# Rotary sum on GpSimd instead of VectorE, and the scaling of the keys at the end of VectorE's iteration

## The chip, the cores and the metric

One core of one Trainium2 chip runs the kernel. The metric is the device time of one execution in microseconds (us). The kernel before was run three times: 747.37 us is the median, 747.22 the lowest and 750.02 the highest.

## What is computed

The kernel is one decoder layer over 32 sequences of 112 rows of 256 numbers. It has three blocks, each with a layer norm before it and a residual sum behind it: attention with 8 heads of 128, attention-like weighing of a context of 375 rows with a gelu, and a quantised feed-forward block with 1,024 hidden units. The change touches the attention:

```python
q = _rmsnorm(einsum('bim,mhd->bhid', x, wq)); k = _rmsnorm(einsum('bim,mhd->bhid', x, wk))
even, odd = split(q, 2, axis=-1)            # the same for k
q = concatenate([even * cos - odd * sin, even * sin + odd * cos], axis=-1)
s = einsum('bhid,bhjd->bhij', q * mult, k * mult)
```

The norm of a head is one factor for each row and head, so the kernel turns first and scales afterwards.

## The kernel before, in words

One sequence is one unit of work, and four sequences are in flight. Each engine has its own hand-written program. `iterations` (line 252) runs its `body(i)` 35 times: three special first ones (FIRST, SECOND, THIRD), a loop unrolled by four, and a drain. Within an iteration, `a` is the sequence whose projections are made, `b` the one before it (scores, softmax, values, output projection), `c` the one before that (context and hidden units), `d` the oldest (its last product), `n` and `m` the next two. Every engine works through its list strictly in order, so a wait holds all that is behind it. The engines are tied together by semaphores only.

The way of the keys `k` of sequence `a` (w = 1; the queries are w = 0):

- TensorE projects them (line 909) into the banks `k_ps`. ScalarE squares them (line 718), and VectorE sums the squares by head (`sum_squares`, line 474, in two halves for the keys).
- VectorE multiplies by the cosines (`turn_cos`, line 482, into `turn_c`) and, with the halves swapped, by the sines (`turn_sin`, line 491, into `turn_s`). `turn` (line 498) adds both into `turn_c`: 112 partitions x 1,024 numbers.
- GpSimd turns the sums of squares into factors in `rms_root` (line 349 adds the epsilon, line 351 raises to -0.5).
- VectorE scales the keys in `normalise_k` (line 503). ScalarE scales the queries in `normalise_q` (line 774) in two halves of four instructions each.
- At the start of the next iteration TensorE waits in `transpose_qk` (line 914) for the scaled queries, transposes their eight heads (line 917), waits for the scaled keys (`k_normed`) and transposes theirs. Only then does it begin the next projection.

The end of an iteration, engine by engine. TensorE ends with `project_out(range(HH, H), b)` (line 1094), twelve products (line 876), the last of which raises `y_ready`. VectorE ends with `split_oT(1, b)` (line 557), `turn(1, a)` (line 662), `split_xnT(n)` (line 433), `normalise_k(a)` (line 666), `residual_attention(b)` (line 568, which waits for `y_ready`; its sum is line 570), `layer_stats` for `b` and `m` (lines 402 to 415) and `clip_hidden(c)` (line 564). GpSimd's order in an iteration is `split_ctx(c)` (line 355), `mask_later_keys(b)` (line 367), `rms_root(0, a)`, `root(2, c)` (line 344), `rms_root(1, a)`, `add_b2(c)` (line 360), `root(1, b)` and `root(0, m)`. The middle of VectorE's iteration has `gelu_outer(c)` (line 515), `turn(0, a)` (line 638), `split_g(c)` (line 530), `turn_cos(1, a)`, ..., where `split_g` waits for a copy by ScalarE and gives TensorE the input of `ctx_out(c)`.

The loads and stores go through SyncE's queue: it stores `y_out` after `out_done`, loads a context after `ctx_lo_done` and a block of x after `x2_done`. No DMA is issued from GpSimd's or VectorE's queue.

Of the kernel before, what the change touches and what calls it, by code (L numbers as in the profile page):

```python
# [29 lines left out]
ALU = mybir.AluOpType  # L30
# [38 lines left out]
def done(j):  # L69

    return j.base + j.off + 1
# [12 lines left out]
def decoder_layer(nc, x, ctx_rows, wq, wk, wv, wo, w1, b1, w2, b2, tables, out):  # L84
# [15 lines left out]
    with ExitStack() as stack:  # L100
# [224 lines left out]
        @block.gpsimd  # L325
        def _(pool):
            pool.memset(nhalf[:, :], -0.5).then_inc(const_done, 1)
            pool.memset(ln_eps[:, :], LN_EPS).then_inc(const_done, 1)
            pool.memset(rms_eps[:, :], RMS_EPS / QK_LIFT ** 2).then_inc(const_done, 1)
            pool.memset(v_sb[:, :, D:VW], 1.0).then_inc(const_done, 1)  # L330
            pool.memset(pool_cell[:, :], 0.0).then_inc(const_done, 1)
            pool.wait_ge(const_done, 5)

            def carry_wait():

                pool.tensor_tensor(pool_cell[:, :], pool_cell[:, :], pool_cell[:, :], ALU.mult)

            def root(n, j):

                if n < 2:  # L340
                    pool.wait_ge(mv_done[n], done(j))
                    pool.tensor_tensor(ve[n][:, :], mv[n][:, 1:2], ln_eps[:, :], ALU.add).then_inc(ve_done[n], 1)
                pool.wait_ge(ve_done[n], done(j))
                pool.tensor_tensor(rstd[n][:, :], ve[n][:, :], nhalf[:, 0:1], ALU.pow).then_inc(rstd_done[n], 1)  # L344

            def rms_root(w, j):

                pool.wait_ge(qk_summed[w], done(j))
                pool.tensor_tensor(ms[:, w, :], ss[:, w, :], rms_eps[:, :], ALU.add).then_inc(qk_ms_done[w], 1)
                pool.wait_ge(qk_ms_done[w], done(j))  # L350
                pool.tensor_tensor(rms[:, w, :], ms[:, w, :], nhalf[:, 0:H], ALU.pow).then_inc(qk_rms_done[w], 1)  # L351

            def split_ctx(j):
                pool.wait_ge(ctx_hi_done, done(j))
                pool.tensor_tensor(ctx_lo[:, :, :], ctx_in[:, j.off % 2], ctx_hi[:, :, :].bitcast(F32),  # L355
                                   ALU.subtract).then_inc(ctx_lo_done, 1)

            def add_b2(j):
                pool.wait_ge(x3_done, done(j))
                pool.tensor_tensor(x3b[:, :], x3[:, :], b2_rows[:, :], ALU.add).then_inc(x3b_done, 1)  # L360

            def mask_later_keys(j):

                pool.wait_ge(exp_done, done(j))
                carry_wait()
                p = p_sb.rearrange("k (h t) -> k h t", h=H)
                pool.affine_select(out=p, in_=p, compare_op=ALU.is_ge, fill=0.0, base=0,
                                   pattern=[[0, H], [1, T]], channel_multiplier=-1).then_inc(p_done, 1)

            def body(i):  # L370
                a, b, c, d, n, m = i, i.plus(-1), i.plus(-2), i.plus(-3), i.plus(1), i.plus(2)
                A, B_, C, D_, N, M_ = (j.inside(B) for j in (a, b, c, d, n, m))
                if i is FIRST:
                    root(0, n)
                if B_ and not A:
                    mask_later_keys(b)
                if C:
                    split_ctx(c)
                if B_ and A:
                    mask_later_keys(b)  # L380
                if A:
                    rms_root(0, a)
                if C:
                    root(2, c)
                if A:
                    rms_root(1, a)
                if C:
                    add_b2(c)
                if B_:
                    root(1, b)  # L390
                if M_:
                    root(0, m)

            iterations(pool, body)


        @block.vector
        def _(dve):
# [92 lines left out]
                dve.tensor_tensor(turn_s[:, w, :].rearrange("t (h two f) -> t h two f", two=2, f=HALF),  # L491
                                  halves, table, ALU.mult).then_inc(sin_done[w], 1)

            def turn(w, j):

                dve.wait_ge(cos_done[w], done(j))
                dve.wait_ge(sin_done[w], done(j))
                dve.tensor_tensor(turn_c[:, w, :], turn_c[:, w, :], turn_s[:, w, :], ALU.add).then_inc(qk_turned[w], 1)  # L498

            def normalise_k(j):  # L500
                dve.wait_ge(k_turned, done(j))
                dve.wait_ge(k_rms_done, done(j))
                dve.tensor_tensor(heads(qkn[:, 1, :]), heads(turn_c[:, 1, :]),
                                  rms[:, 1, :].unsqueeze(2).broadcast_to([T, H, D]), ALU.mult).then_inc(k_normed, 1)
# [75 lines left out]
            def body(i):  # L580
                a, b, c, d, n, m = i, i.plus(-1), i.plus(-2), i.plus(-3), i.plus(1), i.plus(2)
                A, B_, C, D_, N, M_ = (j.inside(B) for j in (a, b, c, d, n, m))
                if i is FIRST:
                    wait_x(n)
                    layer_stats(x_rows(n))
                    normalise_x(n)
                    split_xnT(n)
                    for w in range(3):
                        split_projection(w)
                    dve.wait_ge(ident_in, 16)  # L590
                    dve.tensor_copy(ident_b[:, :], ident[:, :]).then_inc(ident_b_done, 1)
                    wait_x(m)
                    layer_stats(x_rows(m))
                    return
                if i is SECOND:
                    normalise_x(n)
                    dve.wait_ge(table_in, 32)
                    turn_cos(0, a)
                    turn_sin(0, a)
                    sum_squares(0, a).then_inc(q_summed, 1)  # L600
                    split_xnT(n)
                    turn(0, a)
                    sum_squares(1, a).then_inc(k_summed, 1)
                    turn_cos(1, a)
                    turn_sin(1, a)
                    turn(1, a)
                    normalise_k(a)
                    clip_weights(0)
                    return
                if B_:  # L610
                    split_qkT(0, b)
                if i is THIRD:
                    split_wo(0)
                if C and A:
                    normalise_x2(c)
                if B_:
                    split_qkT(1, b)
                if C and not A:
                    normalise_x2(c)
                if i is THIRD:  # L620
                    wait_x(n)
                    layer_stats(x_rows(n))
                    clip_weights(1)
                    fixed_biases()
                if D_:
                    residual_out(d)
                if A:
                    turn_cos(0, a)
                    turn_sin(0, a)
                    sum_squares(0, a).then_inc(q_summed, 1)  # L630
                if C:
                    gelu_inner(c)
                if N:
                    normalise_x(n)
                if C:
                    gelu_outer(c)
                if A:
                    turn(0, a)
                if C:
                    split_g(c)  # L640
                if A:
                    turn_cos(1, a)
                if B_:
                    invert_sums(b)
                if A:
                    turn_sin(1, a)
                if i is THIRD:
                    split_wo(1)
                if C:
                    residual_ctx(c)  # L650
                if A:
                    sum_squares(1, a, slice(0, HH))
                if B_:
                    split_oT(0, b)
                if C:
                    quantise_x3(c)
                if A:
                    sum_squares(1, a, slice(HH, H)).then_inc(k_summed, 1)
                if B_:
                    split_oT(1, b)  # L660
                if A:
                    turn(1, a)
                if N:
                    split_xnT(n)
                if A:
                    normalise_k(a)
                if B_:
                    residual_attention(b)
                if M_:
                    wait_x(m)  # L670
                if B_:
                    dve.wait_ge(x2_done, done(b))
                if B_ or M_:
                    layer_stats(*([x2_rows(b)] if B_ else []), *([x_rows(m)] if M_ else []))
                if C:
                    clip_hidden(c)

# [448 lines left out]
```

## Time and profile before

| what | value |
|---|---|
| median of three runs (lowest, highest) | 747.37 us (747.22, 750.02) |
| span of the profiled execution | 745.4 us |
| TensorE matmuls busy | 714.9 us, 96% |
| VectorE busy | 655.2 us, 88% |
| ScalarE busy | 548.8 us, 74% |
| GpSimd busy | 308.1 us, 41% |
| mean granted clock of TensorE | 0.985 |

The span goes from the first to the last instruction of the one execution that was profiled. Its own total is not given beside it; the median of the runs is 1.97 us above the span. In the rows below PE is TensorE's matmul side, PEld its weight loads, DVE VectorE, ACT ScalarE and POOL GpSimd. L909 is line 909. The granted clock is a share of full speed: 1.00 is 2.4 GHz, 0.50 is 1.2 GHz.

### The profile page before, as it was taken

What the parts mean: (1) busy time and instruction counts of PE and PEld (TensorE: products, weight loads), DVE (VectorE), ACT (ScalarE), POOL (GpSimd) and SP (SyncE); (2) the same over time, 40 slices, a digit from 0 to 9 for tenths busy, and PEclk for the clock granted to TensorE, in tenths of its full rate; (3) what the DMA queues carried; (4) which work ended last, traced back from release to release, by engine and by line L of the source; (5) the groups of instructions that cost most, each with busy time, mean ns of one, the idle gap of its engine ahead of it and who ended that gap; (6) DMA issues with size and microseconds to landing.
All of it is one profiled execution on the core that took longest, in us unless ns stands there. A gap on an engine that the chain in (4) does not pass through costs nothing.

```text
span 745.4 us, 15919 instructions
## 1 busy us (share of the span) xinstructions
PE 714.9 (96%) x5824; PEld 633.9 (85%) x5824; DVE 655.2 (88%) x1264; ACT 548.8 (74%) x1324; POOL 308.1 (41%) x425
## 2 busy tenths in 40 slices
PE   5799999999999999999999999999999999999974
PEld 4588988888888989898898989889898988889863
DVE  6989989999999999999999999999999999998942
ACT  5777777778777777787777878777787777778752
POOL 1335434543443453344344344444434444443421
PEclk9799999999999999999999999999999999999996
DMA  7400011100101100000110000101000011100000
GB/s 264 157 8 28 28 36 34 31 17 28 33 27 33 33 24 21 27 31 29 33 33 19 26 27 27 33 33 33 15 30 27 27 33 34 33 11 20 28 7 12
DMA packets 15371, 26.58 MB, mean 36 GB/s; under 512 B 1536, under 2 KB 10192, under 8 KB 15216
## 3 DMA queue, kind: packets, MB, share of 16 engines
q1 hardware_dynamic: 15344, 26.22, 10.7%
q8 instruction: 17, 0.28, 0.2%
q14 instruction: 10, 0.08, 0.0%
HBM read 22.55 MB, written 3.67 MB: 35 GB/s over the span
## 4 chain that ended last, share of the span: by engine, by line
PE 90%; DVE 3%; ACT 3%; issue 2%; DMA 1%; POOL 1%; SPq 0%; POOLq 0%; DVEq 0%; ACTq 0%
PE psum L909 34%; PE psum L876 22%; PE psum L937 7%; PE psum L917 6%; PE psum L982 6%; PE psum L1013 4%; PE psum L1005 3%; PE psum L944 3%; PE psum L972 3%; PE psum L965 2%; DMA w_raw<-in_wv 1%; ACT qkn L774 1%; ACT w_raw L764 1%; PE psum L997 1%; DVE qkT_lo L550 0%
## 5 line engine op out<-in xcount | busy, mean ns | idle before, releaser
L909 PE MATMUL psum<-wqkv_hi,xnT_hi 128*112 128x512 f32 x384 | 159.3, 415 | 4.4 <-DVE wqkv_lo L440 2.7
L909 PE MATMUL psum<-wqkv_lo,xnT_hi 128*112 128x512 f32 x384 | 151.3, 394 | 0.0
L909 PE MATMUL psum<-wqkv_hi,xnT_lo 128*112 128x512 f32 x384 | 131.8, 397 | 0.0
L344 POOL TENSOR_TENSOR rstd<-ve,nhalf 112x1 f32<-112x1 f32 x96 | 55.4, 577 | 145.8 <-DVE ve L414 140.8
L351 POOL TENSOR_TENSOR rms<-ms,nhalf 112x8 f32<-112x8 f32 x64 | 107.2, 1676 | 5.0
L718 ACT ACTIVATE sq<-psum 112x1024 f32<-112x1024 f32 x64 | 65.0, 1016 | 56.4 <-PE psum L909 56.4
L355 POOL TENSOR_TENSOR ctx_lo<-ctx_in,ctx_hi 125x768 fp32r<-125x768 f32 x32 | 58.6, 1830 | 95.9 <-ACT ctx_hi L684 95.9
L764 ACT ACTIVATE w_raw<-psum,rden 112x128 f32<-112x128 f32 x256 | 69.7, 384 | 26.6 <-DVE rden L525 26.5
L909 PEld LDWEIGHTS psum<-wqkv_hi,xnT_lo 128*112 128x112 f32 x384 | 67.3, 175 | 22.4
L909 PEld LDWEIGHTS psum<-wqkv_hi,xnT_hi 128*112 128x112 f32 x384 | 67.7, 176 | 19.8 <-issue 3.1
L774 ACT ACTIVATE qkn<-turn_c,rms 112x128 f32<-112x128 f32 x256 | 81.5, 400 | 1.4 <-POOL rms L351 1.4
L474 DVE TENSOR_REDUCE ss<-sq 112x4 f32<-112x512 f32 (+1 forms) x95 | 81.8, 861 | 0.0
L909 PEld LDWEIGHTS psum<-wqkv_lo,xnT_hi 128*112 128x112 f32 x384 | 67.9, 177 | 15.1
L482 DVE TENSOR_TENSOR turn_c<-psum,cos_t 112x1024 f32<-112x1024 f32 x64 | 77.8, 1216 | 2.2 <-ACT sq L718 2.2
L876 PE MATMUL psum<-wo_hi,oT_hi 128*112 128x256 f32 x256 | 78.8, 308 | 0.8 <-DVE oT_lo L557 0.8
L498 DVE TENSOR_TENSOR turn_c<-turn_c,turn_s 112x1024 f32<-112x1024 f32 x64 | 77.9, 1217 | 0.1
L491 DVE TENSOR_TENSOR turn_s<-psum,sin_t 112x1024 f32<-112x1024 f32 x64 | 77.3, 1208 | 0.0
L876 PE MATMUL psum<-wo_lo,oT_hi 128*112 128x256 f32 x256 | 72.1, 282 | 0.0
L876 PE MATMUL psum<-wo_hi,oT_lo 128*112 128x256 f32 x256 | 71.8, 281 | 0.0
L550 DVE TENSOR_TENSOR qkT_lo<-psum,qkT_hi 128x896 f16<-128x896 f32 x64 | 69.2, 1082 | 0.2 <-ACT qkT_hi L684 0.2
L788 ACT ACTIVATE f_int<-psum,b_col 128x112 int16<-128x112 f32 x256 | 65.9, 371 | 1.8 <-PE psum L1005 1.8
L937 PE MATMUL psum<-v_sb,w_raw 112*112 112x129 f32 x512 | 62.0, 273 | 0.0
(99 smaller groups left out, 1792.2 us busy)
## 6 DMA issues: line engine op xcount, KB each, us to landing
ctx_in<-in_ctx_rows SPq DMA_DIRECT2D x32, 375.0 KB
x_in<-in_x SPq DMA_DIRECT2D x32, 112.0 KB, 2.0
out_y<-y_out SPq DMA_DIRECT2D x32, 112.0 KB, 1.9
w_raw<-in_w SPq DMA_DIRECT2D x2, 1024.0 KB, 6.2
w_raw<-in_wq SPq DMA_DIRECT2D x2, 512.0 KB, 4.5
w_raw<-in_wk SPq DMA_DIRECT2D x2, 512.0 KB, 6.1
w_raw<-in_wv SPq DMA_DIRECT2D x2, 512.0 KB, 7.8
w_raw<-in_wo SPq DMA_DIRECT2D x1, 1024.0 KB, 10.3
```

The costliest lines, as they stand in the source:

```text
L351: pool.tensor_tensor(rms[:, w, :], ms[:, w, :], nhalf[:, 0:H], ALU.pow).then_inc(qk_rms_done[w], 1)
L474: return dve.tensor_reduce(ss[:, w, hs], heads(sq[:, w, :])[:, hs, :], AX_X, ALU.add)
L482: dve.tensor_tensor(turn_c[:, w, :].rearrange("t (b h d) -> t b h d", b=2, d=D), (q_ps, k_ps)[w].rearrange("t b (h d) -> t b h d", d=D), c ...
L491: dve.tensor_tensor(turn_s[:, w, :].rearrange("t (h two f) -> t h two f", two=2, f=HALF), halves, table, ALU.mult).then_inc(sin_done[w], 1)
L498: dve.tensor_tensor(turn_c[:, w, :], turn_c[:, w, :], turn_s[:, w, :], ALU.add).then_inc(qk_turned[w], 1)
L550: dve.tensor_tensor(qkT_lo[:, w, :].rearrange("p (b n) -> p b n", b=2), (qT_ps, kT_ps)[w], qkT_hi[:, w, :].rearrange("p (b n) -> p b n", b=2),
L764: last = act.activation(on[:, h * D:(h + 1) * D], o_ps[:, h // OH, (h % OH) * VW:(h % OH) * VW + D], ACT.Copy, scale=rden[:, h:h + 1])
L774: last = act.activation(qkn[:, 0, h * D:(h + 1) * D], turn_c[:, 0, h * D:(h + 1) * D], ACT.Copy, scale=rms[:, 0, h:h + 1])
L788: last = act.activation(f_int[:, c * T:(c + 1) * T], f_ps[:, c // (FC // 2), (c % (FC // 2)) * T:(c % (FC // 2) + 1) * T], ACT.Relu, bias= ...
L876: product = pe.matmul(dst, lh, rh, start=first and k == 0, stop=last and k == len(terms) - 1)
L909: last = pe.matmul(ps[:, n, :], left[:, c, :], right[:, c, w, n * BANK:(n + 1) * BANK], start=c == 0 and left is xnT_hi and right is wqkv_ ...
L937: last = pe.matmul(o_ps[:, h // OH, at:at + VW], p_sb[:, h * T:(h + 1) * T], v_sb[:, h, :], start=h % OH == 0, stop=h % OH == OH - 1 or h ...
```

## The change

The function `turn` moves from VectorE's program to GpSimd's. GpSimd calls it for the queries behind `rms_root(0, a)` and for the keys behind `rms_root(1, a)`. VectorE's calls go. `normalise_k(a)` moves from its place before `residual_attention(b)` to the place behind `layer_stats` and before `clip_hidden(c)`. In the special iteration SECOND only the calls of `turn` go. TensorE's, ScalarE's and SyncE's programs stay as they are. The diff:

```diff
--- before.py
+++ after.py
@@ -343,6 +343,12 @@
                 pool.wait_ge(ve_done[n], done(j))
                 pool.tensor_tensor(rstd[n][:, :], ve[n][:, :], nhalf[:, 0:1], ALU.pow).then_inc(rstd_done[n], 1)
 
+            def turn(w, j):
+
+                pool.wait_ge(cos_done[w], done(j))
+                pool.wait_ge(sin_done[w], done(j))
+                pool.tensor_tensor(turn_c[:, w, :], turn_c[:, w, :], turn_s[:, w, :], ALU.add).then_inc(qk_turned[w], 1)
+
             def rms_root(w, j):
 
                 pool.wait_ge(qk_summed[w], done(j))
@@ -380,10 +386,12 @@
                     mask_later_keys(b)
                 if A:
                     rms_root(0, a)
+                    turn(0, a)
                 if C:
                     root(2, c)
                 if A:
                     rms_root(1, a)
+                    turn(1, a)
                 if C:
                     add_b2(c)
                 if B_:
@@ -490,12 +498,6 @@
                 table = sin_t[:, :].rearrange("t (two f) -> t two f", two=2).unsqueeze(1).broadcast_to([T, H, 2, HALF])
                 dve.tensor_tensor(turn_s[:, w, :].rearrange("t (h two f) -> t h two f", two=2, f=HALF),
                                   halves, table, ALU.mult).then_inc(sin_done[w], 1)
-
-            def turn(w, j):
-
-                dve.wait_ge(cos_done[w], done(j))
-                dve.wait_ge(sin_done[w], done(j))
-                dve.tensor_tensor(turn_c[:, w, :], turn_c[:, w, :], turn_s[:, w, :], ALU.add).then_inc(qk_turned[w], 1)
 
             def normalise_k(j):
                 dve.wait_ge(k_turned, done(j))
@@ -599,11 +601,9 @@
                     turn_sin(0, a)
                     sum_squares(0, a).then_inc(q_summed, 1)
                     split_xnT(n)
-                    turn(0, a)
                     sum_squares(1, a).then_inc(k_summed, 1)
                     turn_cos(1, a)
                     turn_sin(1, a)
-                    turn(1, a)
                     normalise_k(a)
                     clip_weights(0)
                     return
@@ -634,8 +634,6 @@
                     normalise_x(n)
                 if C:
                     gelu_outer(c)
-                if A:
-                    turn(0, a)
                 if C:
                     split_g(c)
                 if A:
@@ -658,12 +656,8 @@
                     sum_squares(1, a, slice(HH, H)).then_inc(k_summed, 1)
                 if B_:
                     split_oT(1, b)
-                if A:
-                    turn(1, a)
                 if N:
                     split_xnT(n)
-                if A:
-                    normalise_k(a)
                 if B_:
                     residual_attention(b)
                 if M_:
@@ -672,6 +666,8 @@
                     dve.wait_ge(x2_done, done(b))
                 if B_ or M_:
                     layer_stats(*([x2_rows(b)] if B_ else []), *([x_rows(m)] if M_ else []))
+                if A:
+                    normalise_k(a)
                 if C:
                     clip_hidden(c)
 
```

## Rows read from the trace of the kernel before

**Rows 1.** The page: span, busy times, and the granted clock in 40 slices.

```profile
span 745.4 us, 15919 instructions
...
PE 714.9 (96%) x5824; PEld 633.9 (85%) x5824; DVE 655.2 (88%) x1264; ACT 548.8 (74%) x1324; POOL 308.1 (41%) x425
...
PEclk9799999999999999999999999999999999999996
```

**Rows 2.** The chain that ended last, its longest pieces: start, duration, work.

```profile
384.91 2.79 PE psum L909 x12
406.77 2.79 PE psum L909 x12
```

**Rows 3.** Groups of instructions: busy us, mean ns of one, idle before it.

```profile
L498 DVE TENSOR_TENSOR turn_c<-turn_c,turn_s 112x1024 f32<-112x1024 f32 x64 | 77.9, 1217 | 0.1
...
L355 POOL TENSOR_TENSOR ctx_lo<-ctx_in,ctx_hi 125x768 fp32r<-125x768 f32 x32 | 58.6, 1830 | 95.9 <-ACT ctx_hi L684 95.9
...
L360 POOL TENSOR_TENSOR x3b<-x,b_rows 112x256 f32<-112x256 f32 x32 | 23.6, 737 | 0.0
```

**Rows 4.** Line 503 alone: shortest, median and longest ns, first and last start.

```profile
L503 DVE TENSOR_TENSOR qkn<-turn_c,rms x32: 1212/1540/1689, 26.5 to 703.6; 112x1024 f32<-112x1024 f32 x32
```

**Rows 5.** Timeline of TensorE where one iteration ends: start, duration, instruction.

```profile
420.37 0.28 PE L876 MATMUL psum<-wo_hi,oT_lo 128*112 128x256 f32 x1
...
420.38 1.60 PEld L917 LDWEIGHTS psum<-ident,qkn 112*128 112x128 f32 x16
```

**Rows 6.** Timeline of VectorE at the same iteration's end.

```profile
419.48 1.53 DVE L503 TENSOR_TENSOR qkn<-turn_c,rms 112x1024 f32<-112x1024 f32 x1
420.94 0.41 DVE L570 TENSOR_TENSOR x<-psum,x_in 112x256 f32<-112x256 f32 x1
...
422.34 0.43 DVE L564 TENSOR_SCALAR f_q<-f_int 128x448 bf16<-128x448 int16 x2
```

**Rows 7.** Timeline of GpSimd at the same iteration's end.

```profile
417.58 1.65 POOL L351 TENSOR_TENSOR rms<-ms,nhalf 112x8 f32<-112x8 f32 x1
419.20 0.73 POOL L360 TENSOR_TENSOR x3b<-x,b_rows 112x256 f32<-112x256 f32 x1
```

**Rows 8.** Timeline at VectorE's wait for TensorE, in the drain.

```profile
723.68 0.28 PE L876 MATMUL psum<-wo_hi,oT_lo 128*112 128x256 f32 x1
...
723.99 0.42 DVE L570 TENSOR_TENSOR x<-psum,x_in 112x256 f32<-112x256 f32 x1 [2.86 <-PE psum L876]
```

**Rows 9.** Timeline of the same iteration's middle: GpSimd, VectorE, TensorE's loads, ScalarE.

```profile
408.70 1.65 POOL L351 TENSOR_TENSOR rms<-ms,nhalf 112x8 f32<-112x8 f32 x1
...
409.33 0.49 ACT L684 ACTIVATE g_hi<-g 125x336 fp32r<-125x336 f32 x1 [0.57 <-DVE g L515]
...
410.35 0.50 DVE L530 TENSOR_TENSOR g_lo<-g,g_hi 125x336 fp32r<-125x336 f32 x1
...
411.71 0.17 PEld L876 LDWEIGHTS psum<-ctx_hi,g_hi 125*112 125x112 f32 x1
...
415.77 1.27 ACT L774 ACTIVATE qkn<-turn_c,rms 112x128 f32<-112x128 f32 x4
```

**Rows 10.** Timeline of the special iteration SECOND: the queries' root and their scaling.

```profile
20.68 2.58 POOL L351 TENSOR_TENSOR rms<-ms,nhalf 112x8 f32<-112x8 f32 x1
...
23.35 2.45 ACT L774 ACTIVATE qkn<-turn_c,rms 112x128 f32<-112x128 f32 x8 [1.43 <-POOL rms L351]
```

**Rows 11.** TensorE's stops: timeline, with the idle time before in brackets.

```profile
20.67 0.49 PE L909 MATMUL psum<-wqkv_hi,xnT_hi 128*112 128x512 f32 x1 [1.63 <-DVE xnT_lo L433]
...
25.94 1.58 PE L917 MATMUL psum<-ident,qkn 112*128 112x112 f32 x8 [2.23 <-ACT qkn L774]
...
732.25 0.37 PE L876 MATMUL psum<-ctx_hi,g_hi 125*112 125x256 f32 x1 [3.19 <-DVE g_lo L530]
```

**Rows 12.** Stretches of 0.25 us: busy by engine, then granted clock (PEclk).

```profile
26.00:26.25 0.25, 0.25 (x3) 0.25 (x4) 0.25 (x1) 0.25 (x1) 0.00 (x0) 0.73 0.32 123
...
36.25:36.50 0.25, 0.25 (x7) 0.25 (x5) 0.25 (x1) 0.00 (x0) 0.25 (x2) 0.79 0.00 0
```

## The prediction

> **What bounds the kernel now.** I read the page first. TensorE's matmul side is busy 96% of the span, VectorE 88%, GpSimd 41%, and the granted clock stands at nine tenths or more in all slices but one [rows 1]. The chain that ended last says the same: its longest piece, the twelve products of the key projection, returns after 406.77 - 384.91 = 21.86 us [rows 2], and the pieces between are TensorE's too. So an iteration lasts as long as TensorE's list, which runs there without a stop. VectorE saves nothing by being faster unless TensorE waits for it, and anything that makes TensorE stop is added in full.
>
> The next view is the timeline at the end of one iteration. TensorE's last output product starts at 420.37 and ends at 420.65; its weight loads for the 16 transposes follow at once, from 420.38 to 421.98 [rows 5]. The first eight are the queries', so the keys' begin at 420.38 + 1.60 / 2 = 421.18. VectorE had scaled the keys from 419.48 to 421.01, before it took the residual sum at 420.94 [rows 6]. The scaled keys are just there when TensorE wants them.
>
> **Removed: two sums on VectorE.** They are 64 instructions of 1,217 ns, 77.9 us in all, 2.43 us per iteration [rows 3]. On the path that sets the end they are worth nothing, since the steady iteration has no stop of TensorE for VectorE to shorten. The freed time becomes waiting.
>
> **Added: two sums on GpSimd.** No row has this size. Two sums and differences of the same engine are near: 768 columns take 1,830 ns and 256 take 737 ns [rows 3]. The slope is (1,830 - 737) / 512 = 2.13 ns per column, so 1,024 columns take 1,830 + 256 x 2.13 = 2,376 ns; in plain proportion to the larger row it would be 2,440 ns. I take 2.38 us. That is 152 us more for GpSimd, 460 us of some 745, so it does not become the bound by its total.
>
> For the queries, the root ends at 408.70 + 1.65 = 410.35, the sum at 412.7, and ScalarE begins to scale them at 415.77 [rows 9]: hidden, with 3 us to spare. For the keys, the root ends at 417.58 + 1.65 = 419.23 and the sum at 421.61 [rows 7]. Behind it stand `add_b2` and both last roots. The roots need statistics that end near 422.1 even now, so they move by the 0.73 us of `add_b2` [rows 7] at most, and what they feed (`normalise_x2`, then `normalise_x`) is not wanted by TensorE until after its next projection. I cost that at nothing.
>
> **Moved: the scaling of the keys.** This is the term that counts. Behind `layer_stats`, it stands behind `residual_attention`, whose wait is for TensorE's last product of the iteration. So the chain is closed: TensorE ends its list, VectorE does the residual sum, statistics and scaling, and TensorE, having transposed the queries, must wait for it. Step by step:
>
> - VectorE starts the residual sum 0.03 us after the product's end, as it did in the drain, where it was really waiting (723.68 + 0.28 = 723.96, start 723.99) [rows 8]. Here: 420.68.
> - From the start of that sum to the start of what follows the statistics takes 422.34 - 420.94 = 1.40 us [rows 6]. The scaling starts at 422.08. GpSimd's sum, done at 421.61, is 0.47 us early.
> - The scaling takes 1.21 us at least, 1.54 in the median and 1.69 at most [rows 4]. The instance at 419.48 took 1.53, and GpSimd's `add_b2` ran beside it until 419.93 [rows 6, 7]: 0.45 us beside each other cost 0.32. After the change `add_b2` runs from 421.61 to 422.34, beside the scaling for 0.26 us, so I take 1.21 + 0.19 = 1.40. It ends at 423.48, and with 0.03 us for the release TensorE goes on at 423.51.
>
> The stop is 423.51 - 421.18 = 2.33 us. The bounds are 2.14 us (scaling 1.21) and 2.62 us (1.69). It comes at the start of every iteration whose keys were scaled in the new place, sequences 1 to 31: 31 x 2.33 = 72 us, between 66 and 81. Nothing wins it back, since TensorE's list has no other stop. `clip_hidden`, queued behind the scaling, is 1.4 us later against TensorE, but is first wanted after the next projection. No DMA moves; SyncE's waits are for results ahead of the scaling.
>
> The Trainium skill, on the page "SBUF — State Buffer" in the section "SBUF: two separate sides", says that GpSimd and a VectorE instruction with two SBUF inputs take turns on a shared pair of ports, and that the later one is held until the other's whole instruction is done. By that, the scaling would start only at 422.34 and run 1.21 us, and the stop would be 2.40 us instead of 2.33; the slow instance above agrees with it roughly (held 0.32 us where the rule says 0.45).
>
> **The start.** In SECOND both sums go before the first key and query transposes. There the queries' root took 2.58 us from 20.68 and ScalarE began at 23.35 [rows 10]. I take 1.65 us for the root now that no sum on VectorE runs beside it, then 2.38: 24.71, some 1.4 us later; with the root still at 2.58 it would be 2.3 us. The keys' sum is another GpSimd sum behind. I take 2 us for the start, between 1 and 4.
>
> **The clock.** The stops that matter are long for it. TensorE stopped for 2.23 us before 25.94 [rows 11], and the granted clock went from 1.00 to 0.50 in the stretch after 26.00, to come back only in the one after 36.25 [rows 12]. A stop of 1.63 us before 20.67 brought no fall; one of 3.19 us in the drain, before 732.25, did [rows 11], by the last slice of the page. The new stop lies at the edge. [...] How many stops bring a fall these rows don't say: between none and 31, so 0 to 56 us. Since the two stops over 2.2 us did and the 1.63 us one did not, and the new one is barely over, I take one in five: 6 x 1.8 = 11 us.
>
> **The sum.** On the profiled execution: 745.4 + 72 + 2 + 11 = 830.4 us of span. The median of the runs is 1.97 us above that span, so the time is 832.5 us.
>
> **The rivals.**
>
> 1. *The clock falls in most iterations.* For it: both stops over 2.2 us were followed by a fall [rows 11, 12]. Against it: they are two, in the start and the drain, with other stops near them, while here 22 us of full work surround each. All 31 give 821.5 + 56 = 877 us, half of them 849. Chance 0.24.
> 2. *GpSimd's sum of the queries holds VectorE.* ScalarE's copy of `g_hi` ends at 409.82, and `split_g` waited until 410.35 only because the sum was before it on VectorE [rows 9]. Now it can start at 409.85, half a microsecond before GpSimd's sum at 410.35. If the order turns round and the sum holds it until 412.7, it ends at 413.2, where TensorE wants it at 411.71 [rows 9]: a second stop of 1.5 us, 31 x 1.5 = 47 us on 821.5 to 832.5, some 870 to 880. The page named above is the rule by which it would. It decides from a delay of 0.5 us. Chance 0.05.
> 3. *GpSimd's sum of the keys is the late one.* Its cover is 422.08 - 419.23 = 2.85 us. If the sum takes 3.6 us, as it would if VectorE slowed it by half, each stop grows by 0.8 us: 25 us more, 857 us. Chance 0.05.
> 4. *The other side: no slower, or faster.* This needs the scaling to end before 421.18, that is to start by 420.0, while its queue is held until 420.68. Then only the relief of VectorE would be left, and what it can win is the two stops of TensorE behind VectorE in the start and drain, 1.63 and 3.19 us [rows 11]: 747.4 - 4.8 = 742.6 us. For it speaks only that VectorE is at 88%. Chance 0.03.
>
> **How the numbers follow.** The forecast, a stop of 2.1 to 2.6 us with few falls, has 0.63 and its own range 813 to 850. Rival 1 fills 849 to 880, where rivals 2 and 3 lie too. The range from 812 to 880 leaves out rival 4 and the tails, under 2 in 10. About 0.5% is what a measurement can tell from no change: faster by more than that 0.02, within it 0.01, slower 0.97.
>
> **What would show it.** TensorE idle before a line 917 load in each iteration, released by VectorE's line 503, some 2.3 us and 31 times; line 498 on GpSimd near 2.4 us; VectorE idle before line 570 for TensorE; the distance of the projections near 24.2 us where the clock stands at full. More than ten stretches of clock 0.50 in the body would show rival 1, an idle TensorE before the context products rival 2, and line 503 released by GpSimd rival 3. A steady distance still near 21.9 us would prove me wrong altogether.

## The result and the profile after

The changed kernel takes 824.06 us in the median of four runs (822.43 to 825.46), against 747.3 us for the kernel before. The ratio is 1.1023, with a 95% interval of 1.0996 to 1.105: it is 10% slower. The profiled run took 825.35 us, its span 823.6.

These lines of the page answer to [rows 1 and 3]. The last two come from the full list of groups of instructions (out<-in, shapes, count, busy us, mean ns, idle before it and its releaser).

```profile
span 823.6 us, 15919 instructions
...
PE 728.9 (88%) x5824; PEld 639.5 (78%) x5824; DVE 587.2 (71%) x1200; ACT 551.8 (67%) x1324; POOL 493.3 (60%) x489
...
PEclk9899999999999999999999999999999999999995
...
PE 80%; DVE 11%; issue 3%; POOL 2%; ACT 2%; DMA 1%; SPq 0%; POOLq 0%; DVEq 0%
...
L350 POOL TENSOR_TENSOR turn_c<-turn_c,turn_s 112x1024 f32<-112x1024 f32 x64 | 153.7, 2402 | 0.0
L913 PEld LDWEIGHTS psum<-ident,qkn 112*128 112x128 f32 x512 | 53.3, 144 | 74.7 <-DVE qkn L505 69.1 <-issue 5.6
L505 DVE TENSOR_TENSOR qkn<-turn_c,rms 112x1024 f32<-112x1024 f32 x32 | 41.0, 1281 | 5.2 <-POOL turn_c L350 5.2
```

VectorE lost 68 us of busy time, and TensorE fell from 96% busy to 88%. The fourth line is the chain that ended last, by engine: VectorE now holds 11% of it, where it held 3%. The row to see is the second last. The loads of the transposes waited 69.1 us for the scaled keys (line 505 is the old line 503). The kernel before has 0.3 us there. Its two lines are:

```profile
PE 90%; DVE 3%; ACT 3%; issue 2%; DMA 1%; POOL 1%; SPq 0%; POOLq 0%; DVEq 0%; ACTq 0%
...
L917 PEld LDWEIGHTS psum<-ident,qkn 112*128 112x128 f32 x512 | 52.3, 143 | 3.7 <-issue 3.3 <-DVE qkn L503 0.3
```

How this looks within an iteration stands in its timeline. The first fence is VectorE's, the second GpSimd's, the third the loads of TensorE. They answer to [rows 5 to 7].

```profile
392.92 0.42 DVE L572 TENSOR_TENSOR x<-psum,x_in 112x256 f32<-112x256 f32 x1 [2.25 <-PE psum L872]
...
394.34 1.27 DVE L505 TENSOR_TENSOR qkn<-turn_c,rms 112x1024 f32<-112x1024 f32 x1
395.54 0.45 DVE L566 TENSOR_SCALAR f_q<-f_int 128x448 bf16<-128x448 int16 x2
```

```profile
391.46 2.39 POOL L350 TENSOR_TENSOR turn_c<-turn_c,turn_s 112x1024 f32<-112x1024 f32 x1
393.81 0.73 POOL L366 TENSOR_TENSOR x3b<-x,b_rows 112x256 f32<-112x256 f32 x1
394.49 1.54 POOL L342 TENSOR_TENSOR ve<-mv,ln_eps 112x1 f32<-112x1 f32 x1
```

```profile
392.61 0.83 PEld L913 LDWEIGHTS psum<-ident,qkn 112*128 112x128 f32 x8
395.67 0.78 PEld L913 LDWEIGHTS psum<-ident,qkn 112*128 112x128 f32 x8 [2.23 <-DVE qkn L505]
...
419.75 0.78 PEld L913 LDWEIGHTS psum<-ident,qkn 112*128 112x128 f32 x8 [2.20 <-DVE qkn L505]
```

VectorE had nothing to do for 2.25 us, since it waited for TensorE's last output product. Then the residual sum, 1.42 us to the scaling's start (394.34 - 392.92), 1.27 us of scaling, and 0.06 us later TensorE goes on. Each waits for the other, one after the other. From one key transpose to the next it is 419.75 - 395.67 = 24.08 us. Before, an iteration was 21.86 to 21.87 us [rows 2], so the stop adds 2.21 us.

The granted clock, read in stretches of 0.8 us: the kernel before has no stretch below 1.00 between 36.8 and 732.0. The changed one has five short ones in the body, from about 53.6, 77.6, 128.8, 347.2 and 589.6, each some 3.4 us at 0.50. Two stretches of the first (busy times by engine, then PEclk):

```profile
54.40:55.20 0.80, 0.80 (x3) 0.60 (x2) 0.37 (x1) 0.40 (x1) 0.00 (x0) 0.50 0.00 0
56.80:57.60 0.80, 0.80 (x4) 0.55 (x4) 0.00 (x0) 0.00 (x0) 0.00 (x0) 0.72 0.00 0
```

TensorE is fully busy in both, the first at half rate and the second while the clock comes back. At 1.2 instead of 2.4 GHz, 3.4 us would do the work of 1.7. What a fall cost can be measured: with the one at 347.2, it is 371.60 - 345.98 = 25.62 us from one load of the keys' transposes to the next, against 24.08 without. So a fall costs 1.54 us.

**Where the 78.2 us of span went.** The residual sum (line 570 before, 572 after) divides both spans. From its first to its last instance it was 673.9 us before and is 751.1 us now: 77.2 more. The 31 stops make 69.1 us of it (most are of 2.21 us, four of 2.31 to 2.49) and the five falls 5 x 1.54 = 7.7, together 76.8. Before the first instance it is 0.3 us less (50.1, now 49.8), behind the last 1.3 us more (21.4, now 22.7).

### The profile page after: what moved, and what is told of

It is laid out like the page before. It is cut to its first block, busy times and chain, and to the rows that moved or that the text cites. A ratio compares the mean times of both kernels' runs of the same rounds, so it can differ in the third digit from the quotient of the medians.

```text
span 823.6 us, 15919 instructions
## 1 busy us (share of the span) xinstructions
PE 728.9 (88%) x5824; PEld 639.5 (78%) x5824; DVE 587.2 (71%) x1200; ACT 551.8 (67%) x1324; POOL 493.3 (60%) x489
## 4 chain that ended last, share of the span: by engine, by line
PE 80%; DVE 11%; issue 3%; POOL 2%; ACT 2%; DMA 1%; SPq 0%; POOLq 0%; DVEq 0%
PE psum L905 31%; PE psum L872 20%; PE psum L933 7%; PE psum L978 5%; DVE qkn L505 5%; PE psum L913 4%; PE psum L1009 3%; PE psum L1001 3%; PE psum L940 3%; PE psum L968 2%; DVE stat L413 2%; DVE x L572 2%; PE psum L961 1%; DMA w_raw<-in_wv 1%; POOL turn_c L350 1%
## 5 line engine op out<-in xcount | busy, mean ns | idle before, releaser
L905 PE MATMUL psum<-wqkv_hi,xnT_hi 128*112 128x512 f32 x384 | 162.4, 423 | 4.1 <-DVE wqkv_lo L448 2.7
L905 PE MATMUL psum<-wqkv_lo,xnT_hi 128*112 128x512 f32 x384 | 154.8, 403 | 0.0
L350 POOL TENSOR_TENSOR turn_c<-turn_c,turn_s 112x1024 f32<-112x1024 f32 x64 | 153.7, 2402 | 0.0
L905 PE MATMUL psum<-wqkv_hi,xnT_lo 128*112 128x512 f32 x384 | 133.6, 402 | 0.0
L913 PE MATMUL psum<-ident,qkn 112*128 112x112 f32 x512 | 63.6, 269 | 67.5 <-DVE qkn L505 63.9
L913 PEld LDWEIGHTS psum<-ident,qkn 112*128 112x128 f32 x512 | 53.3, 144 | 74.7 <-DVE qkn L505 69.1
L357 POOL TENSOR_TENSOR rms<-ms,nhalf 112x8 f32<-112x8 f32 x64 | 105.5, 1648 | 5.0
L680 ACT ACTIVATE qkT_hi<-psum 128x896 f16<-128x896 f32 x64 | 60.0, 937 | 66.3 <-PE psum L913 66.2
L905 PEld LDWEIGHTS psum<-wqkv_hi,xnT_lo 128*112 128x112 f32 x384 | 69.2, 180 | 23.5
L905 PEld LDWEIGHTS psum<-wqkv_hi,xnT_hi 128*112 128x112 f32 x384 | 69.1, 180 | 20.2 <-issue 3.1
```

The source lines that it names most:

```text
L350: pool.tensor_tensor(turn_c[:, w, :], turn_c[:, w, :], turn_s[:, w, :], ALU.add).then_inc(qk_turned[w], 1)
L905: last = pe.matmul(ps[:, n, :], left[:, c, :], right[:, c, w, n * BANK:(n + 1) * BANK], start=c == 0 and left is xnT_hi and right is wqkv_ ...
L913: last = pe.transpose((qT_ps, kT_ps)[w][:, h // HH, (h % HH) * T:(h % HH + 1) * T], qkn[:, w, h * D:(h + 1) * D], ident[0:T, 0:T])
```

## The experiments

All ratios are to the kernel before, on the same chip. The theory was that the loss is the closed chain from TensorE's last product to the keys' transposes. The rivals were GpSimd's sums as the cost, VectorE's relief as a gain, and the clock.

### One part alone

**The move without GpSimd.**

```diff
+                if A:
+                    normalise_k(a)      # before clip_hidden(c); its call before residual_attention(b) goes
```

> Both sums stay on VectorE; only the scaling of the keys moves behind the statistics. Theory (the loss is the closed chain from TensorE's last product over residual sum, statistics and scaling to the keys' transposes): the stop is again 1.42 us to the scaling's start, 1.22 to 1.25 us of scaling and 0.05 of release, 2.2 us, and the time 820 to 827 us with 4 to 7 falls of the clock. Rival (the sums on GpSimd cost most of it): under 785 us. Rival (the clock alone): the stop remains but no falls: 815 us.

Measured: 817.14 us, ratio 1.094 (1.0922 to 1.0958). VectorE and TensorE's loads in its timeline:

```profile
413.40 0.42 DVE L570 TENSOR_TENSOR x<-psum,x_in 112x256 f32<-112x256 f32 x1 [1.13 <-PE psum L876]
...
414.82 1.20 DVE L503 TENSOR_TENSOR qkn<-turn_c,rms 112x1024 f32<-112x1024 f32 x1
...
416.08 0.78 PEld L917 LDWEIGHTS psum<-ident,qkn 112*128 112x128 f32 x8 [2.16 <-DVE qkn L503]
```

The stop is 2.16 us and there are four falls in the body of the profiled execution. The time came 3 us under the range I had given. The move alone makes 70 of the 77 us. The part of the change that has to do with GpSimd is not needed for the loss.

**GpSimd's sums without the move.**

```diff
# the changed kernel, with normalise_k(a) before residual_attention(b) again
```

> Both sums on GpSimd, the scaling of the keys at its old place, before the residual sum. Theory: the scaling now waits for GpSimd's sum, done about 2.4 us after the keys' root; TensorE would have gone on at 1.2 us before that sum's end in the old timing, so a stop of 1.7 us or more per iteration: 800 us without falls of the clock. If add_b2, which GpSimd begins in the same moment, holds the scaling as it did in the kernel before, the stop is 2.2 us: 815 to 825 us. Rival (VectorE's relief pays and only the move hurts): 742 to 750 us.

Measured: 822.09 us, ratio 1.101 (1.0991 to 1.1028). Its GpSimd and VectorE:

```profile
410.49 2.38 POOL L350 TENSOR_TENSOR turn_c<-turn_c,turn_s 112x1024 f32<-112x1024 f32 x1
412.84 0.73 POOL L366 TENSOR_TENSOR x3b<-x,b_rows 112x256 f32<-112x256 f32 x1
```

```profile
412.91 1.73 DVE L505 TENSOR_TENSOR qkn<-turn_c,rms 112x1024 f32<-112x1024 f32 x1 [3.19 <-POOL turn_c L350]
```

The stop is 2.19 us, now set by GpSimd: VectorE waits 3.19 us for the keys' sum. And the scaling takes 1.73 us instead of 1.2, because `add_b2` on GpSimd began 0.07 us before it. So either part of the change alone costs nearly what both cost together. They overlap: with both, GpSimd's sum is ready at 393.85, just before the residual chain asks for it at 394.34.

**Only the queries' sum on GpSimd.**

```diff
+                    turn(0, a)          # GpSimd, behind rms_root(0, a)
-                if A:
-                    turn(0, a)          # VectorE; the keys' sum and the scaling stay
```

> Only the queries' sum goes to GpSimd, the keys' sum and the scaling stay as before. Theory: it is covered by 3 us and TensorE has no stop to shorten: 746 to 750 us, with VectorE 39 us less busy. Rival (GpSimd's sum holds VectorE's split of g, or delays the third norm): over 765 us. Rival (relief of VectorE pays): under 743 us.

Measured: 748.49 us, ratio 1.0021 (1.0008 to 1.0033). From the first to the last residual sum it takes 673.9 us, exactly as before, and the start is 1.3 us longer (51.4 against 50.1). This half of the transfer is hidden in the body, as far as TensorE goes, and VectorE's relief brings nothing. The 1.3 us of the start come from one profiled execution of each kernel.

### The length of the chain

**Scaling before the statistics, sums on VectorE.**

```diff
                 if B_:
                     residual_attention(b)
+                if A:
+                    normalise_k(a)
```

> Both sums on VectorE; the scaling stands behind the residual sum but before the statistics. Theory: the chain is shorter by the statistics, the scaling starts 0.35 to 0.5 us after the residual sum's start, and the stop is 1.1 to 1.3 us: 781 to 788 us, and the clock falls only in the start and the drain. Rival (the stop has another length-giver than that chain): the same 815 to 827 us as with the scaling last.

Measured: 780.44 us, ratio 1.0446 (1.0428 to 1.0463). The time is half a microsecond under the range I had given. The residual sum starts at 416.71 and the scaling at 417.05:

```profile
416.71 0.42 DVE L570 TENSOR_TENSOR x<-psum,x_in 112x256 f32<-112x256 f32 x1 [1.13 <-PE psum L876]
417.05 1.22 DVE L503 TENSOR_TENSOR qkn<-turn_c,rms 112x1024 f32<-112x1024 f32 x1
...
418.31 0.78 PEld L917 LDWEIGHTS psum<-ident,qkn 112*128 112x128 f32 x8 [1.09 <-DVE qkn L503]
```

The chain is 1.07 us shorter and so is the stop. From the first to the last residual sum it takes 708.0 us, 34.1 more than before; 31 x 1.09 = 33.8. No fall of the clock in the body.

**Scaling behind the clip as well.**

```diff
                 if C:
                     clip_hidden(c)
+                if A:
+                    normalise_k(a)      # its call before clip_hidden(c) goes
```

> The changed kernel with the scaling also behind the clip of the hidden units, so that the chain is longer by the clip's 0.36 us. Theory: stop 2.57 us, 31 x 0.36 = 11 us more, and more falls of the clock in the body (8 to 14 instead of 5), in all 838 to 852 us. Rival (the clock does not care for 0.36 us): 833 to 837 us. Rival (something else is the length-giver): no change.

Measured: 842.7 us, ratio 1.1297 (1.1268 to 1.1325).

```profile
426.33 0.78 PEld L913 LDWEIGHTS psum<-ident,qkn 112*128 112x128 f32 x8 [2.57 <-DVE qkn L505]
```

The stop is 2.57 us and the clock falls ten times in the body. The 31 stops make 80.0 us and the falls 10 x 1.54 = 15.4, together 95.4; the middle part grew by 769.4 - 673.9 = 95.5. The clock does care: 0.36 us more in each stop doubled the falls, and the mean granted clock of the four executions is 0.958 to 0.966, against 0.974 to 0.977 in the changed kernel.

### What GpSimd and VectorE do to each other

**`add_b2` ahead of the keys' root.**

```diff
+                if C:
+                    add_b2(c)
                 if A:
                     rms_root(1, a)
                     turn(1, a)          # normalise_k(a) at its old place
-                if C:
-                    add_b2(c)
```

> Both sums on GpSimd, the scaling at its old place, and GpSimd's add_b2 ahead of the keys' root instead of behind their sum. Theory (add_b2 holds the scaling for 0.5 us): the scaling takes 1.22 us instead of 1.73, the stop is 1.7 us, and the time 797 to 803 us. Rival (the scaling is slow for another reason, for instance because it starts right behind GpSimd's sum): 1.73 us again, 818 to 824 us.

Measured: 802.4 us, ratio 1.0746 (1.0718 to 1.0774). Line 505 alone, shortest, median and longest ns, and the stop:

```profile
L505 DVE TENSOR_TENSOR qkn<-turn_c,rms x32: 1225/1226/1227, 29.0 to 760.1; 112x1024 f32<-112x1024 f32 x32
...
431.22 0.78 PEld L913 LDWEIGHTS psum<-ident,qkn 112*128 112x128 f32 x8 [1.71 <-DVE qkn L505]
```

With nothing of GpSimd's beside it the scaling never takes more than 1.23 us. That alone is worth 20 us in the whole. The cause of the slow scalings is shown. Two falls in the body remain.

**The same, with the scaling between residual sum and statistics.**

```diff
                 if B_:
                     residual_attention(b)
+                if A:
+                    normalise_k(a)      # its call before residual_attention(b) goes
```

> Both sums on GpSimd, add_b2 ahead of the keys' root, the scaling behind the residual sum and before the statistics. Theory: now the keys' sum on GpSimd ends last, 0.6 us behind the residual sum, and sets the stop: 1.7 us, 797 to 803 us, released through VectorE by GpSimd's sum. Rival (the residual sum sets it, as with the sums on VectorE): stop 1.1 us, 779 to 784 us.

Measured: 803.63 us, ratio 1.0747 (1.0729 to 1.0765), 0.6 us above the range I had given.

```profile
429.23 0.42 DVE L572 TENSOR_TENSOR x<-psum,x_in 112x256 f32<-112x256 f32 x1 [2.26 <-PE psum L872]
430.18 1.23 DVE L505 TENSOR_TENSOR qkn<-turn_c,rms 112x1024 f32<-112x1024 f32 x1 [0.52 <-POOL turn_c L350]
```

The stop is 1.71 us again, not the 1.09 us that the same place gives with the sums on VectorE. The residual chain would have let the scaling start 0.52 us sooner; GpSimd's sum did not. So at both places tried with `add_b2` first, the keys' sum on GpSimd costs 1.7 us per iteration with this order on TensorE. Whether GpSimd could have it ready sooner in another order of its own was not tried.

**Keys transposed behind the next projection.**

```diff
# TensorE, the changed kernel
                 if B_ and i is not THIRD:
                     pe.wait_ge(v_copied, half(b, 1))
                     transpose_qk(0, b)
-                    transpose_qk(1, b)
...
                     project(0, a, q_ps, q_ready)
+                if B_ and i is not THIRD:
+                    transpose_qk(1, b)
```

> The changed kernel, but TensorE transposes the keys behind the next projection of the queries (2.8 us of work) instead of before it. Theory (TensorE wants the keys 2.2 us too early): the stop before the keys' transposes goes, since the work in between is longer than the stop; the keys' split then reaches the scores late by 0.9 us, so 770 to 780 us, and the clock falls only in the start and the drain. Rival (the stop is VectorE's or GpSimd's queue being late as a whole): 815 to 827 us as before.

Measured: 828.66 us, ratio 1.1108 (1.1079 to 1.1136). Both the theory's 770 to 780 and my picture of what would follow were wrong. The stop before the keys' transposes did go. The middle of the iteration shows what came (VectorE, then GpSimd, then TensorE's loads):

```profile
403.45 2.69 DVE L532 TENSOR_TENSOR g_lo<-g,g_hi 125x336 fp32r<-125x336 f32 x1 [0.55 <-ACT g_hi L680]
...
403.42 2.36 POOL L350 TENSOR_TENSOR turn_c<-turn_c,turn_s 112x1024 f32<-112x1024 f32 x1
...
406.19 0.17 PEld L872 LDWEIGHTS psum<-ctx_hi,g_hi 125*112 125x112 f32 x1 [0.55 <-DVE g_lo L532]
...
416.28 0.17 PEld L905 LDWEIGHTS psum<-wqkv_hi,xnT_hi 128*112 128x112 f32 x1 [0.61 <-ACT f_int L784]
422.29 0.13 PEld L872 LDWEIGHTS psum<-qkT_hi 128*112 128x112 f16 x1 [1.34 <-issue]
```

GpSimd's sum of the queries began 0.03 us before the split of g, and the split took 2.69 us instead of 0.51. That is the prediction's second rival, in another kernel than the one for which it was stated. In its place TensorE stops three times per iteration for more than 0.5 us. The iteration is 427.91 - 403.45 = 24.46 us long (the next split starts at 427.91).

**The same, with GpSimd's sum behind the split.**

```diff
                     rms_root(0, a)
+                    if C:
+                        pool.wait_ge(g_lo_done, done(c))
                     turn(0, a)
```

> As with the keys transposed later, and GpSimd's sum of the queries also waits for VectorE's split of g, which costs it half a microsecond. Theory (in that run GpSimd's sum began 0.03 us before the split and held it for 2.2 us, and that held turn_cos, the inverted sums, ScalarE and in the end TensorE in two places): the split takes 0.51 us again, the stops before the context products and before the queries' projection go, only the one before the scores stays, 0.9 to 1.2 us, and the time is 775 to 790 us. Rival (later transposes of the keys cost the 80 us by themselves): 820 us or more.

Measured: 805.1 us, ratio 1.0785 (1.0749 to 1.0821). The split's line alone, and two loads of TensorE:

```profile
L534 DVE TENSOR_TENSOR g_lo<-g,g_hi x32: 507/507/510, 61.9 to 789.0; 125x336 fp32r<-125x336 f32 x32
...
405.81 0.17 PEld L907 LDWEIGHTS psum<-wqkv_hi,xnT_hi 128*112 128x112 f32 x1 [0.44 <-ACT f_int L786]
411.82 0.13 PEld L874 LDWEIGHTS psum<-qkT_hi 128*112 128x112 f16 x1 [1.34 <-issue]
```

The hold is gone, with 23.6 us of the time; that it was the hold is shown. But I had expected 775 to 790. Two stops stay. One is 1.34 us before the scores, where I had worked out 0.9. The keys' transposes only begin at 408.47 there, and between them and the scores stand ScalarE's copy (409.67 to 410.59) and VectorE's split (410.62 to 411.71), for which TensorE never waited in the body of the kernel before. The other is 0.44 us before the queries' projection, which now comes 0.8 us sooner and meets ScalarE still at the hidden units. Together 1.78 us, and with 21.87 that is the 23.7 us which an iteration now lasts.

**The keys' part alone in that order.**

```diff
# keys' sum on GpSimd, scaling last, keys transposed later; turn(0, a) back on VectorE before split_g(c)
```

> The keys' sum on GpSimd, the scaling last and the keys transposed later, but the queries' sum back on VectorE. Theory: without GpSimd's sum of the queries nothing holds the split of g, so the same as with the sum behind the split: 775 to 790 us. Rival (the keys' part alone makes the loss of the run with later transposes): 820 us or more.

Measured: 805.42 us, ratio 1.0779 (1.0746 to 1.0813), the same as the run before it, as the theory said, and again not at the 775 to 790 it named. The split takes 0.50 us. The stops are 0.44 and 1.33 us.

No version here beats the kernel before. The nearest is the queries' sum alone on GpSimd, 0.2% slower. In the steady iteration the kernel before leaves nothing to win by VectorE, as TensorE's list has no stop in it.

## Why the prediction was right, step by step

The forecast was 832.5 us, the result is 824.06, in the range of the likeliest case. By its own steps:

- **The sums removed from VectorE.** Costed at nothing. That is right: the run with the queries' sum alone on GpSimd has the same middle part, 673.9 us.
- **The sums added on GpSimd.** Taken at 2.38 us, measured 2.39 in the median (2.36 to 2.56). The Trainium skill, on the page "GPSIMD Engine Reference" in the section "3.1 Elementwise — side-by-side cycle accounting", gives a ratio of 1.96 between GpSimd and VectorE for a longer fp32 sum; here it is 2.39 / 1.217 = 1.96, too. Being 0.47 us early was right: 0.49 us (393.85 to 394.34). GpSimd's total was forecast at 460 us and is 493.3. Most of the rest is its one-column sum (line 342), held beside the scaling: 52.0 us where it was 14.7. For that reason the root of `b` ends 3.78 us behind TensorE's last product (at 396.66) instead of 2.61, which is 1.17 us later and not 0.73 at most. TensorE does not stop for it.
- **The chain.** 1.40 us to the scaling's start was 1.42, the release 0.03 was 0.06. The scaling was the mis-sized term: 1.40 taken, 1.25 us in the median and 1.27 in the iteration shown. I had put 0.26 us of `add_b2` beside it and let it cost 0.19. It was beside it for 0.17 to 0.20 us and cost 0.03 to 0.05 over the 1.22 of the shortest scaling. So the stop was 2.21 and not 2.33 us, in all 69.1 us for 72. Line 505 alone, shortest, median and longest ns:

```profile
L505 DVE TENSOR_TENSOR qkn<-turn_c,rms x32: 1224/1251/1731, 28.9 to 780.6; 112x1024 f32<-112x1024 f32 x32
```

- **The start.** Taken as 2 us, measured -0.3 us. The queries' scaling did start 1.3 us later (24.68 against 23.35, [rows 10]) and the keys' transposes at 30.27. But the low clock of the start was over by 33.6 instead of 36.8, which can have paid for it; that is argued, not shown. In the run with the scaling before the statistics and `add_b2` first, whose start is the same, the low clock lasted until 36.5 and the first residual sum came at 50.4. In the runs with the scaling moved and both sums on VectorE, whose start is the old one, it came at 49.0 and 50.0. So 2 us was too much, and what the start costs is not told from nothing.
- **The clock.** Six falls for 11 us, measured five for 7.7. No row of the kernel before shows the 1.8 us that the sum takes for a fall: the one low stretch in its start lasted about 10 us, from the stretch after 26.00 to the one after 36.25 [rows 12]. The falls in the body lasted 3.4 us and cost 1.54. The edge was read from idle times of matmuls, 2.23 and 1.63 us [rows 11], and set against a stop of the loads. Measured on the matmuls the new stop is 2.00 us in the median, so it is not over the stops that brought a fall but between them and the one that did not. The count was an estimate, and that it came near is luck in part: three of the five falls came at stops that were longer than the usual 2.21 us, and the runs with stops of 2.16, 2.19, 2.21 and 2.57 us have 4, 4, 5 and 10 falls.
- **The drain.** Not priced. It was 1.3 us longer: the granted clock falls at 804.8, 3.9 us behind the last residual sum, and before it did so 8.7 us behind.

Together the sum was 830.4 us of span against 823.6. It was too high by 2.9 for the stops, 3.3 for the clock and 2.3 for the start, and too low by 1.3 for the drain. The other 0.4 us are those of the middle part that stops and falls leave open. The median of the runs lies a further 1.6 us under the forecast, mostly since the profiled execution, at 825.35 us, was one of the two slower ones.

Of the rivals, the first (falls in most iterations) did not happen: five falls in 31 iterations. The fourth (no slower) fell with the queries' run. The third (the keys' sum late) did not happen in the changed kernel but waited half a microsecond behind it: the run with both sums on GpSimd, `add_b2` first and the scaling before the statistics met it. The second needed 0.5 us to turn the order round: in the changed kernel the split of g starts at 382.13 and GpSimd's sum at 382.60. One other change on TensorE turned it round.

## What to carry to other kernels

An instruction that the bottleneck engine wants at the start of its next round must not be queued behind a wait for the last thing that it does in this round: the whole chain between the two is then paid in every round, whatever is saved on the engine that runs it. Before moving an instruction, write down when its reader wants it and which wait each new place puts before it. And a transfer to a slower engine can be hidden at one place and not at another: the queries' sum had 3 us of cover and cost 0.2%, the keys' sum had none.

## What the runs showed of the hardware

**GpSimd's sums and VectorE hold each other, GpSimd's root does not.** An instruction of VectorE with two inputs in SBUF that starts while GpSimd runs its sum of the queries or `add_b2` is held to about the other's end. The split of g: 2.69 us, started 0.03 us behind GpSimd's sum, against 0.51. The scaling: 1.73 us when `add_b2` was 0.07 us old, 1.53 when it was 0.28 us old [rows 6, 7], 1.25 when it was 0.56 us old, and 1.20 to 1.23 with nothing beside it. Line 490 of the changed kernel (`turn_cos`), which has one input in PSUM, is the check: 30 times it started inside GpSimd's sum and took 1.22 to 1.23 us, as otherwise.

It goes the other way too: GpSimd's one-column sum on line 342 takes 1.54 us when it starts inside the scaling, and 0.20 in the median. At 394.49 it ended at 396.03, which is 0.42 us behind the scaling's end; the clip ran on VectorE in that time (395.54 to 395.99), and whether it held the sum as well was not tried.

But not every instruction of GpSimd holds one of VectorE's. In the changed kernel the split of g started 30 times inside the queries' root, up to 0.5 us before its end, and took 0.51 us:

```profile
380.99 1.65 POOL L357 TENSOR_TENSOR rms<-ms,nhalf 112x8 f32<-112x8 f32 x1
...
382.13 0.51 DVE L532 TENSOR_TENSOR g_lo<-g,g_hi 125x336 fp32r<-125x336 f32 x1 [0.55 <-ACT g_hi L680]
```

The Trainium skill, on the page "SBUF — State Buffer" in the section "SBUF: two separate sides", describes an exclusive lock held for the whole instruction. For GpSimd's sums the traces agree with it, but for 0.13 to 0.15 us: the split ended at 406.14, while the sum's end at 405.78 and its own 0.51 us would give 406.29. For the root they do not.

**The granted clock answers to short stops, but not to the shortest.** In the body, TensorE is otherwise fully busy. These are the stops of its loads at the keys' transposes, and the falls of one profiled execution each:

| run | usual stop | falls in the body, and the stops at which they came |
|---|---|---|
| scaling before the statistics, sums on VectorE | 1.09 us | none |
| `add_b2` first | 1.71 us | two, at 2.48 and 1.91 us |
| the same, scaling before the statistics | 1.71 us | one, at 2.13 us |
| the move without GpSimd | 2.16 us | four, all at 2.16 us |
| GpSimd's sums without the move | 2.19 us | four, three at 2.19 and one at 2.40 us |
| the changed kernel | 2.21 us | five, at 2.49, 2.31 and 2.36 us and two at 2.21 us |
| scaling behind the clip | 2.57 us | ten, one at 2.49 and nine at 2.56 to 2.57 us |

So none of the 31 stops of 1.09 us brought a fall and none of the 56 of 1.70 to 1.72 us; the shortest with one was of 1.91 us. Length alone does not decide: most stops of 2.16 to 2.57 us brought none, nor did two of 2.74 and 2.75 us in the last run of the table. The three runs with the keys transposed later have one fall (at 2.63 us), none, and two (at 2.16 and 2.39 us). Each fall went from 2.4 to 1.2 GHz for some 3.4 us and cost 1.54 us. Why some iterations bring a fall and others with the same stop don't was not tried. The stop of 1.63 us in the kernel before [rows 11] is of matmuls; a stop of 1.71 us of the loads is one of 1.50 us there, so nothing here speaks against it as a length without a fall.
